# Mamba's odd states: their products with B made by ScalarE on turned tiles and put by TensorE into the bank of the decays

## The reference, cut to what matters

```python
def step(h, inp):
    d_t, b_t, c_t, u_t = inp
    dA = jnp.exp(d_t[..., None] * A)
    dBu = d_t[..., None] * b_t[:, None, :] * u_t[..., None]
    h = dA * h + dBu
    y_t = jnp.einsum('bdn,bn->bd', h, c_t)
    return (h, y_t)
```

## Time and profile before

| | us |
|---|---|
| three runs | 1485.15, 1485.25, 1486.59 |
| the profiled execution, its time | 1480.25 |
| its span | 1478.5 |
| PE, DVE, ACT, POOL busy | 1204.4, 983.9, 818.2, 393.3 |
| PEclk, mean granted clock of TensorE | 0.915 of full |

### The profile page before, as it was taken

How to read it: one execution, slowest core, us unless ns; L and a number is a source line. 1 busy time by engine, 2 the same in 40 slices (tenths; PEclk the granted TensorE clock), 3 DMA queues, 4 the chain that set the end, 5 groups by cost and what they waited for, 6 DMA issues and landing times.

```text
span 1478.5 us, 23087 instructions
## 1 busy us (share of the span) xinstructions
PE 1204.4 (81%) x8416; PEld 771.2 (52%) x8416; DVE 983.9 (67%) x1914; ACT 818.2 (55%) x2176; POOL 393.3 (27%) x248
## 2 busy tenths in 40 slices
PE   5967877887899879899885776899778987889895
PEld 3722334785566446656641222478655654565563
DVE  4789997313565679659649999851256668974974
ACT  4256543452576357768746654235347744766873
POOL 0134654314000134013010666351210013311400
PEclk9678999998799989999987999889979989999998
DMA  8210001484000011001010000048600000100100
GB/s 296 86 57 1 0 1 62 133 272 154 1 2 2 1 36 30 9 8 30 9 29 0 1 0 1 0 135 274 200 14 1 2 1 8 26 12 8 30 8 15
DMA packets 42178, 72.20 MB, mean 49 GB/s; under 512 B 3794, under 2 KB 27474, under 8 KB 41811
## 3 DMA queue, kind: packets, MB, share of 16 engines
q1 hardware_dynamic: 40018, 66.53, 14.3%
q0 software_dynamic: 2048, 4.20, 0.9%
HBM read 51.19 MB, written 13.24 MB: 44 GB/s over the span
## 4 chain that ended last, share of the span: by engine, by line
PE 46%; DVE 25%; ACT 15%; issue 7%; POOL 3%; DMA 3%; SPq 0%; DVEq 0%; POOLq 0%; ACTq 0%
DVE scratch L902 6%; PE psum L1331 3%; ACT scratch L1718 3%; PE psum L1553 3%; DVE scratch L894 3%; ACT scratch L1386 3%; PE psum L1313 2%; PE psum L1120 2%; PE psum L1134 2%; PE psum L750 2%; PE psum L957 2%; PE psum L1326 2%; PE psum L1442 2%; PE psum L1349 1%; PE psum L664 1%
## 5 line engine op out<-in xcount | busy, mean ns | idle before, releaser
L931 POOL TENSOR_TENSOR scratch<-scratch 128x1024 f32<-128x1024 f32 x64 | 151.0, 2370 | 199.0 <-DVE scratch L902 182.8
L653 POOL TENSOR_TENSOR small<-small,w_const 128x16 f32<-128x16 f32 x32 | 97.5, 3051 | 252.4 <-DVE small L1762 252.4
L902 DVE TENSOR_TENSOR_SCAN scratch<-psum,scratch 128x512 f32<-128x512 f32 x128 | 150.7, 1208 | 12.6 <-ACT psum L823 12.1
L750 PE MATMUL psum<-scratch,w_const 128*128 128x512 f32 x256 | 142.1, 686 | 15.4 <-POOL scratch L931 15.3
L653 POOL TENSOR_TENSOR rstd<-rstd,w_const 128x4 f32<-128x4 f32 x32 | 32.7, 1026 | 385.3 <-DVE rstd L615 376.9
L823 ACT ACTIVATE psum<-scratch,a_neg 128x512 f32<-128x512 f32 x128 | 88.3, 691 | 77.5 <-DVE scratch L902 67.2
L1386 ACT ACTIVATE scratch<-psum,mx 128x256 f32<-128x256 f32 (+1 forms) x256 | 111.1, 460 | 28.2 <-DVE mx L1423 24.6
L739 PE MATMUL psum<-scratch,cb 96*128 96x512 bf16 x128 | 50.1, 418 | 70.2 <-DVE scratch L894 60.8
L1172 ACT ACTIVATE scratch<-psum,scratch 128x128 f32<-128x128 f32 x240 | 67.5, 373 | 64.3 <-PE psum L1120 64.2
L1423 DVE TENSOR_REDUCE mx<-psum 128x4 f32<-128x1024 f32 (+1 forms) x56 | 68.1, 1221 | 46.3 <-PE psum L1331 46.3
L1718 ACT ACTIVATE scratch<-psum,mx 128x128 f32<-128x128 f32 x256 | 90.7, 400 | 13.0 <-DVE mx L1809 12.9
(11 more groups left out here) (277 smaller groups left out, 3046.9 us busy)
## 6 DMA issues: line engine op xcount, KB each, us to landing
expert_weights<-in_expert_weights SPq DMA_DIRECT2D x61, 512.0 KB, 4.9
scratch<-scratch SPq DMA_DIRECT2D x48, 128.0 KB, 2.3
folded_products<-expert_weights SPq DMA_DIRECT2D x8, 512.0 KB, 2.6
folded<-folded_products SPq DMA_DIRECT2D x8, 512.0 KB, 3.9
w_local<-in_local SPq DMA_DIRECT2D x1, 3122.0 KB
sorted_y<-scratch SPq DMA_DIRECT2D x12, 256.0 KB, 5.4
scratch<-sorted_x SPq DMA_DIRECT2D x4, 704.0 KB, 6.4
scratch<-in_cross SPq DMA_DIRECT2D x1, 2624.5 KB, 12.4
```

The costliest lines, as they stand in the source:

```text
L653: t.eng.tensor_tensor(v, v, W("const", "neg_half").to_broadcast([P, v.shape[1]]), ALU.pow).then_inc(t.s[done], 1)
L750: ins = pe.matmul(sum_banks[c], ident, t.m.hC[:, 2 * ((n - 1) % 2) + c, :], start=(n == 1), stop=(n == NS))
L902: dve.tensor_tensor_scan(t.m.hs[:, n % 2, c, :], t.ps["dA"], t.m.dBu[n % 2][:, c, :], 0.0, ALU.mult, ALU.add)\
L931: t.eng.tensor_tensor(t.m.hC[:, 2 * (n % 2):2 * (n % 2) + 2, :], t.m.hs[:, n % 2], C, ALU.mult)\
```

## The change

For even n nothing is new, except that their product has one buffer instead of two. For odd n:

- ScalarE multiplies du with B where the tokens lie on the partitions, so that B is a number per partition: four instructions of 128 x 256, one per tile of 128 tokens (`scale_by_b`), into `scaled`. For n = 1 they stand together before the state's decays; for later n two stand behind the even state's first decay and two behind its second.
- TensorE turns four tiles of `scaled` for each half (`turn_scaled`) into the bank `dA`, and the scan takes the product from that bank. The turns of a half wait until the scan before has read the bank.
- ScalarE writes the decays of odd n into a scratch buffer (`dAs`), and the scan takes them from there.
- The spread of B (L739) and VectorE's product (L894) are gone.

Once per pass there are new: eight small products that form B with tokens on the partitions (128 x 16 each) and a copy by ScalarE (`bT`); two groups of four turns of du, and two copies of 128 x 512 by ScalarE (`duT`). These buffers use `xT` and `y`, free at that time. `TURNS` is new for every engine: steps of lane 0 and lane 1 go from 792 + 826 to 814 + 848 (pe), 601 + 602 to 639 + 640 (act), 812 + 845 to 796 + 829 (dve); pool has 91 + 90 and sp 63 + 53 in both. Of the table the list of pool is shown here.

```diff
@@ -101,77 +101,77 @@
 TURNS = {
...
     "pool": [
-        7, 2, 7, 1, 1, 1, 1, 1, 1, 2, 1, 1, 1, 3, 2, 2, 1, 1, 1, 1, 1, 1, 1, 2, 1, 3, 1, 2, 1, 4, 3, 3, 3, 1, 2,
-        2, 1, 2, 2, 2, 1, 1, 1, 2, 2, 2, 2, 2, 3, 3, 2, 1, 1, 1, 2, 1, 1, 1, 1, 1, 2, 1, 1, 1, 1, 1, 1, 1, 1, 1,
-        1, 1, 1, 1, 1, 3, 2, 1, 2, 2, 2, 3, 1, 2, 2, 2, 3, 3, 5, 1, 1, 1, 1, 2, 1, 2, 1, 2, 1, 2, 2, 1, 1, 2, 1,
-        1, 1, 1],
+        4, 2, 5, 1, 1, 1, 1, 2, 1, 1, 1, 1, 1, 2, 1, 1, 1, 1, 1, 1, 1, 1, 1, 2, 2, 2, 3, 2, 1, 3, 1, 2, 2, 2, 3,
+        3, 5, 1, 1, 1, 1, 3, 1, 1, 1, 2, 1, 2, 2, 2, 1, 1, 1, 1, 1, 1, 2, 2, 2, 1, 1, 1, 1, 1, 1, 1, 1, 1, 1, 1,
+        1, 1, 1, 1, 1, 1, 1, 1, 1, 1, 1, 1, 1, 1, 1, 1, 1, 2, 3, 2, 2, 1, 1, 2, 1, 2, 2, 2, 3, 3, 3, 1, 2, 2, 1,
+        2, 1, 1, 1, 1, 1, 2, 1, 1, 2, 1, 1, 1, 1, 2, 1, 1],
...
@@ -388,7 +388,10 @@
             m.dBu0, m.Cs, m.hC = carve(i, 2, T), carve(i, 2, T), carve(i, 4, T)
             m.mid = carve(i, T // 2).bitcast(BF16)
             m.parts = carve(i, T // 2).bitcast(BF16)
-            m.dBu = (m.dBu0, carve(i, 2, T))
+            m.scaled = carve(i, NT, NB * P)
+            m.dAs = carve(i, T)
+            m.duT = (m.xT[:, :].rearrange("p (t d) -> p t d", t=2), m.y_flat.rearrange("p (t d) -> p t d", t=2))
+            m.bT = m.small[:, 2:6, :]
             again(i, early)
             m.rest, m.dtS = carve(i, T), carve(i, T)
             again(i, early + 4 * T)
@@ -447,7 +450,7 @@
                      "hot_ready slots_ready blocks_known bias_ready scattered sorted0_loaded sorted1_loaded "
                      "weights0_loaded weights1_loaded weights2_loaded weights3_loaded block_filled block_copied "
                      "sorted_stored gathered0 gathered1 "
-                     "squares_ready rms_ready u_ready soft_ready delta_ready parts_ready decay_ready decay_used state_ready states_used "
+                     "scaled_ready dbu_filled squares_ready rms_ready u_ready soft_ready delta_ready parts_ready decay_ready decay_used state_ready states_used "
                      "sum_filled skip_ready gated_ready gap_ready ratio_ready comb_ready pads_ready "
                      "rinv_ready inverse_ready max_ready vx_loaded ss_ready root_ready halves_ready rope_ready sq_ready rst_ready hn_ready "
                      "y_ready stored ")
@@ -720,6 +723,14 @@
                 ins = pe.matmul(bank[0:96, :], W("mamba", "x_bc", c=NB)[:, c, :], t.m.u[:, c, :],
                                 start=(c == 0), stop=(c == NB - 1))
             ins.then_inc(t.s["v_filled"], 1)
+            yield
+            bank = t.a.open()
+            for i in range(NT):
+                for c in range(NB):
+                    ins = pe.matmul(bank[:, i * NS:(i + 1) * NS], tok(t.m.u[:, c, :], i),
+                                    W("mamba", "x_bc", c=NB)[:, c, 0:NS], start=(i == 0 and c == 0),
+                                    stop=(i == NT - 1 and c == NB - 1), skip_group_check=True)
+            ins.then_inc(t.s["a_filled"], 1)
             for c in range(NB):
                 yield
                 if c == 0:
@@ -727,17 +738,39 @@
                 pe.matmul(t.a.open(), W("mamba", "w_dt")[0:DTR, c * P:(c + 1) * P], t.m.dtS[0:DTR, :],
                           start=True, stop=True).then_inc(t.s["a_filled"], 1)
             sum_banks = [t.a.banks[0], t.a.banks[1]]
+
+            def turn_scaled(n, c):
+                yield
+                if c == 0:
+                    t.w(t.s["scaled_ready"])
+                pe.wait_ge(t.s["decay_used"], NB * (NS * t.row + n) + c)
+                for i in range(NT):
+                    ins = pe.transpose(tok(t.ps["dA"], i), t.m.scaled[:, i, c * P:(c + 1) * P], ident)
+                ins.then_inc(t.s["dbu_filled"], 1)
+
             t.v.use(1)
             for n in range(NS + 1):
+                if n == 1:
+                    for i in (0, 2):
+                        yield
+                        if i == 0:
+                            t.w(t.s["delta_ready"])
+                        bank = t.a.open()
+                        for k in range(4):
+                            ins = pe.transpose(tok(bank, k), tok(t.m.du[:, k % 2, :], i + k // 2), ident)
+                        ins.then_inc(t.s["a_filled"], 1)
                 if n < NS:
-                    for which in (n, NS + n):
+                    if n % 2:
+                        yield from turn_scaled(n, 0)
+                    for which in (n, NS + n)[n % 2:]:
                         yield
                         if which == 0:
                             pe.wait_ge(t.s["cb_loaded"], 16)
                             t.w(t.s["parts_ready"])
-                            pe.wait_ge(t.s["a_freed"], t.a.at)
                         pe.matmul(t.v.open(), cbv["select"][0:96, which:which + 1].to_broadcast([96, P]), t.m.parts[0:96, :],
                                   start=True, stop=True).then_inc(t.s["v_filled"], 1)
+                    if n % 2:
+                        yield from turn_scaled(n, 1)
                 if n == 8:
                     for c in range(NB):
                         yield
@@ -745,6 +778,8 @@
                         pe.matmul(sum_banks[c], ident, t.m.u[:, c, :], start=False, stop=False)
                 if n >= 1:
                     yield
+                    if n == 1:
+                        pe.wait_ge(t.s["a_freed"], t.a.at)
                     t.w(t.s["state_ready"])
                     for c in range(NB):
                         ins = pe.matmul(sum_banks[c], ident, t.m.hC[:, 2 * ((n - 1) % 2) + c, :],
@@ -792,6 +827,9 @@
             yield
             act.activation(t.m.dtS[0:DTR, :], t.a.take()[0:DTR, :], ACT.Copy).then_inc(t.s["a_freed"], 1)
             yield
+            act.activation(t.m.bT.rearrange("p t n -> p (t n)"), t.a.take()[:, 0:NT * NS], ACT.Copy)\
+                .then_inc(t.s["a_freed"], 1)
+            yield
             for c in range(NB):
                 yield
                 bank = t.a.take()
@@ -807,27 +845,52 @@
             t.skip(v=1)
             bank_freed = t.v.at
             t.v.use(1)
+
+            def scale_by_b(n, half):
+                yield
+                if half == 0:
+                    if n == 1:
+                        act.wait_ge(t.s["a_freed"], t.a.at)
+                    if n > 1 or t.row:
+                        act.wait_ge(t.s["dbu_filled"], NS * t.row + n - 1)
+                for i in (2 * half, 2 * half + 1):
+                    ins = act.activation(t.m.scaled[:, i, :], t.m.duT[half][:, i % 2, :], ACT.Copy,
+                                         scale=t.m.bT[:, i, n:n + 1])
+                if half:
+                    ins.then_inc(t.s["scaled_ready"], 1)
+
             for n in range(NS):
+                if n == 1:
+                    for half in range(2):
+                        yield
+                        act.activation(t.m.duT[half].rearrange("p t d -> p (t d)"), t.a.take(), ACT.Copy)\
+                            .then_inc(t.s["a_freed"], 1)
+                    for half in range(2):
+                        yield from scale_by_b(1, half)
                 for c in range(NB):
-                    i = NB * n + c
-                    yield
-                    if i == 0:
+                    yield
+                    if n == 0 and c == 0:
                         if t.row:
-                            t.w.count(t.s["decay_used"], 1)
                             t.w.count(t.s["state_ready"], 2)
                         t.w(t.s["delta_ready"])
                         act.wait_ge(t.s["a_ready"], 2)
                         act.wait_ge(t.s["v_freed"], bank_freed)
-                    else:
-                        t.w(t.s["decay_used"])
-                    act.activation(t.ps["dA"], t.m.delta[:, c, :], ACT.Exp, scale=a_neg[:, c, n:n + 1])\
+                    elif c == 1 or n % 2 == 0:
+                        act.wait_ge(t.s["decay_used"], NB * (NS * t.row + n) + c)
+                    elif n > 1 or t.row:
+                        act.wait_ge(t.s["decay_used"], NB * (NS * t.row + n - 1))
+                    act.activation(t.m.dAs if n % 2 else t.ps["dA"], t.m.delta[:, c, :], ACT.Exp, scale=a_neg[:, c, n:n + 1])\
                         .then_inc(t.s["decay_ready"], 1)
+                    if n % 2 == 0 and n:
+                        yield from scale_by_b(n + 1, c)
                     if c == 0:
-                        t.skip(v=1)
+                        if n % 2 == 0:
+                            t.skip(v=1)
                         yield
+                        bank = t.v.take()
                         if n >= 2:
                             t.w(t.s["state_ready"])
-                        act.activation(t.m.Cs[:, n % 2, :], t.v.take(), ACT.Copy).then_inc(t.s["v_freed"], 1)
+                        act.activation(t.m.Cs[:, n % 2, :], bank, ACT.Copy).then_inc(t.s["v_freed"], 1)
                         if n in (4, 5):
                             yield
```

(35 more changed lines are left out.)

## The result

The changed kernel took 1509.18 us (four runs, 1508.21 to 1510.64) beside 1485.2 for the kernel before: 1.0159 times its time, 95% interval 1.0129 to 1.019. The forecast was 1473, the range 1452 to 1495. Measured twice more, on other chips, the same code gave 1.0141 and 1.0104. It is slower, by 1.0 to 1.6%. All ratios leave out the executions that took over 1.5% more than the fastest of the same kernel.

The account below looks back on a forecast made before the run. VectorE was taken as busiest, full throughout the second Mamba stretch and only partly in the first. VectorE -28, ScalarE's queue +12 and once per pass +4 gave -12, so 1485.25 became 1473 us; range 1452 to 1495.

Parts of the forecast that it names:

- once per pass: Start of each Mamba pass: eight small products behind B, 2.1 us per pass on the chain to delta; +4 us in all.
- the table: New order of steps in the queues: lanes closer together in the first stretch, later stages nearly unchanged; zero, ends -10 and +10.
- VectorE, -28: Odd states' products removed in the Mamba stretches: saves 17.9 us in the second, the chain's 9.7 in the first.
- ScalarE's queue, +12: Pairs of new products ahead of the other lane's decays: one in three of 64 shows 0.56 us.
- What the profile was to show: Profile after: DVE 946, ACT 887, PE above 1230; second stretch's scans 110 to 115 us, their waits 5 to 10.
- TensorE's turns, 0: Turns of scaled products take the place of the decay's write, 0.66 against 0.69 us; two lanes hide them, cost zero.
- The turns and copies of du: Before the decays of n = 1: could stall that scan up to 2 us per pass; counted zero, other end 8.
- Rival D: ScalarE becomes the bound through its queue, ahead of the other lane's decay: slower, 1497 or 1524; chance 0.22.
- Later stages lose or gain over 5 us: Stages after the Mamba stretches: a shift over 5 us was named as a sign that the forecast is wrong altogether.

Follow-up runs that it names:

- narrow: The changed kernel's form of the products behind B, 128x16 each; the changed kernel itself took 1.0159, 1.0141 and 1.0104 times the kernel before.
- e13: Changed kernel with the products behind B 96 columns wide and row 1's later stages in the order before the change: 1486.45 us, ratio 1.0011.
- e10: Kernel before, with the two 512-wide products that form B and C issued twice: 1489.11 us, ratio 1.0025.
- e5: Changed kernel with ScalarE's products for odd states from n = 3 on cut to one single-element instruction per half: 1487.04 us, ratio 1.0084.
- e2: Instructions of the kernel before in the order of the changed kernel: 1505.65 us, ratio 1.0186.
- e1: Changed kernel's instructions with the steps in the order of the kernel before: 1517.84 us, ratio 1.0282.
- wide: Changed kernel with the products that form B 96 columns wide instead of 16, ScalarE copying the 16 wanted: ratios 1.0019, 1.0009 and 0.9984.
- e19: Against e8's form, lane 1's last gate moved earlier on VectorE and its output product earlier on TensorE: 1471.36 us, ratio 1.0001.
- e6: The changed kernel unaltered, measured again on another chip: 1490.23 us, ratio 1.0141.
- e16: The changed kernel unaltered, measured again on a further chip: 1489.74 us, ratio 1.0104.
- e12: e8's form with the 512-wide products for B and C issued twice: 1497.6 us, ratio 1.0077.
- e15: e13 with two of du's eight turns and copies of one element: 1489.97 us, ratio 1.0028.
- e9: Changed kernel with only one of four tiles of B formed by narrow products and copied to all four: 1481.3 us, ratio 1.0042.
- e7: Changed kernel with the products behind B 96 columns wide, on the chip of e6: 1472.0 us, ratio 1.0009.
- e8: Changed kernel with products behind B 96 columns wide and row 1's later stages in the order before the change: 1465.72 us, ratio 0.9963.
- e14: Changed kernel, narrow products kept, only row 1's later stages in the order before the change: 1504.86 us, ratio 1.0145.

## Why the prediction was wrong, point by point

Two steps failed: the term "once per pass" left out the clock of what stands behind the narrow products, and the term "the table" was set to zero where the order costs time.

- **VectorE, -28.** The prices held (busy 952 against a forecast 946), the worth did not. In the second stretch I took all 17.9 us because VectorE had no idle time. From scan 16 to 64 twelve products went, 13.4 us at the 1.12 of the earlier trace rows, and 8.9 came back by the profiles of before and after: once VectorE is no longer full, B's spread (6.9 us of waits) and the decays (7.1) end last. In the first stretch 9.7 less 2 for the pass's start was forecast. The first gates fell from 205.5 to 197.6 in e13, but that is no hit: e13's clock stayed up in 30:63, and that of the kernel before had fallen (0.56). With the clock up the old code had 199.4 (e10, which has the doubled products besides), with the clock down the new code has 208.3 to 210.4. So at a like clock the new code is 1 to 2 us better there or 3 to 5 us worse, by one profile of the old code for each.
- **ScalarE's queue, +12.** Wrong; e5 shows zero in the scans of the second stretch, and at most some 3 us in the first. The pairs stand beside a scan of the other lane. The earlier trace rows were also misread: the copy takes 0.60 and the decay starts 0.62 behind it, so they do not overlap; that two new products take 0.91 and not 0.98 was right without that ground.
- **What the profile was to show.** PE over 1230 held, DVE came within 6 us of its 946, and the scans' waits for the decays and the turns were 9.3 us, inside the 5 to 10 named. ACT came to 866 and not 887: the new products overlap (14.3 us for 32, so 0.447 each, 6 us in all), four table loads of 1.28 us are gone (51 before, 47 after and in e2, 51 in e1, so it is the order's doing), and the other half is not accounted for. ACT and PE were not near 90% of the second stretch but at 77 and 79, and DVE at 84. The scans took 119 us, not 110 to 115.
- **TensorE's turns, 0.** Right in the changed table, where the scans wait 2.2 us for them. In e1's they were the worst wait of all, so the zero belongs to the order and not to the turns.
- **Once per pass, +4.** This is the first step that failed. The products behind B were priced as 2.1 us of queue; they took 1.9 at the upper clock. Not priced was what stands behind them at which clock: wide against narrow is 18 to 20 us on three chips. The earlier trace rows held a group of small products, and nothing in the sum looked at the clock behind it, though the earlier trace rows showed 0.83 and the earlier trace rows 0.71 in the very stretch into which the change put them. The turns and copies of du were rightly zero.
- **The table, 0 with ends of 10.** This is the second. The old code in the new order lost 1.86%, some 27 us, where 10 was the worst end; part of that is again a lower clock (0.912 in the mean against 0.920 beside it). The lanes do start closer together in the first stretch. In the second the new order costs 4.5 to 6.3 us before scan 16 (wide; e2) and about 5 us between last scan and last gate. The first is shown by e2; of the second e2 shows 2.8, and the rest is read from the trace alone, since e19 missed it. I compared the lists by counts of GpSimd's steps, which cannot show a decay that jumps ahead of the other lane's L844 or a gate behind a reduction.
- **Rival D** had the right sign and the wrong cause; that the time came out between its 1497 and 1524 is luck. "Later stages lose or gain over 5 us" was named as what would make the forecast wrong altogether: gates to end took 16.0 us more. But this stretch varies by as much without the change: the same new code took 572.5, 565.3 and 558.5 us for it in its three profiles (after, e6, e16), and the old code 556.5 and 567.0 (before, e10). No run separates the change's part of the 16.0.

Sum for the second pass: -8.9 (scans 16 to 64), +4.5 (start, order), +7.1 (start, narrow: 77.9 against 70.8), +5.2 (gate) = +7.9. The +7.1 is of one pair of profiles: the narrow form had scan 16 at 77.9, 77.9, 74.3 and 72.4, the wide form at 70.8 to 71.6 (e12 and e15 aside), so it is 1 to 7. Without the narrow products the change is where the kernel before is (0.9984 to 1.0019): what VectorE gives back and what the order takes are then about equal.

Still open: at the same granted clock the wide form is slower than before. 48 runs of the kernel before on the chips of e1 to e9 fall on a line of -9.9 us per 0.01 of mean clock, 2.9 us about it; at 0.921 it gives 1473.0, and the other kernels moved along it 1482.1 (e7), 1485.6 (e6) and 1476.2 (e8). The wide form's gain in clock pays for some 9 us that the passes above explain only in part. Open too is what the narrow products cost in the order of before with the rest in its place: e1 is the one run of that kind, and its turns hide it.

## What to carry to other kernels

Before adding small products to TensorE's queue, look at the granted clock of the stretch behind them: if it already dips there, price the work that follows at both levels, and try the products wider, which here cost 0.06 us a group. Work taken from a full engine is worth its length only until the next wait ends last; look for that wait in the trace of before. An order written out by hand is part of a change: run the old code in the new order, and read for each stage's first and last instruction what it now stands behind.

## What the runs showed of the hardware that was not expected

- Sixteen fp32 instructions of 128x16 take 1.86 us and of 128x96 take 1.92 at the upper clock: the width is nearly free, and the wide form was 18 to 20 us faster on three chips.
- TensorE, busy 100% of the time, was granted 0.59 of its clock over 33 us (e14), and 1.00 with 88% busy in the same stretch of e13. Setup groups took 3.68 and 1.98 us at 1.2 GHz, 2.00 and 1.09 at 2.4 GHz.
- One kernel's executions on one chip spread by 1460 to 1496 us with the mean granted clock from 0.935 to 0.904, close to a line. One profile of each can't tell two kernels apart that differ by 1%.
- One chip of four was slower by 13 us for the same kernel (1485 against 1472).
